# A four-layer transformer on one core: in the second layer the query and key projections are issued ahead of the weight turns

## The reference, cut to what matters

```python
# attention: 16 heads of 64, per sequence; a sparse causal mask
q, k, v = split(xn @ w_qkv)
attn = softmax(where(mask, q @ k.T * scale, -inf))
out  = (attn @ v) @ w_out
# ffn: 8 experts, each token weighted by its two best gates
scores = sigmoid(xn @ gate_w.T)
w_t    = scores where the expert is among the top 2 of scores + bias, else 0
out   += sum over e of square(relu((xn * w_t[e]) @ w_up[e].T)) @ w_down[e].T
```

## Time and profile before

| what | number |
|---|---|
| median of 3 runs | 2010.46 us (2008.64 to 2013.45) |
| the profiled execution | 2017.39 us, span 2015.5 us |
| mean granted TensorE clock | 0.961 |
| busy over the span | PE 91%, DVE 70%, ACT 60%, POOL 52% |
| the second layer's steps | about 434 to 1108 us of the span |

### The profile page before, as it was taken

One profiled execution on the slowest core, in us unless ns is written; L12 is line 12 of the kernel. 1 busy time (PEld: TensorE's weight loads), 2 busy tenths in 40 slices (PEclk: granted clock), 3 DMA queues, 4 the chain that ended last, 5 costly groups with the idle time before them and its releaser, 6 DMA issues.

```text
span 2015.5 us, 40795 instructions
## 1 busy us (share of the span) xinstructions
PE 1828.9 (91%) x13210; PEld 1346.1 (67%) x13210; DVE 1407.1 (70%) x4875; ACT 1206.3 (60%) x3496; POOL 1039.7 (52%) x1489
## 2 busy tenths in 40 slices
PE   5788787549999999999999899999998999999998
PEld 2555564337777777777777566666666777777776
DVE  6999974347677676777766766666665777777775
ACT  3445243246666666666665555555555787777885
POOL 3211354838888888887888311111113555555554
PEclk9889689869999999999999999999998999999999
DMA  6100014530311101110110000000000000000000
GB/s 189 34 1 2 2 25 116 94 93 20 126 28 28 27 18 33 28 28 27 18 33 12 21 1 1 1 1 1 1 1 1 5 4 7 7 7 7 7 2 12
DMA packets 74976, 53.66 MB, mean 27 GB/s; under 512 B 7056, under 2 KB 72976, under 8 KB 73872
## 3 DMA queue, kind: packets, MB, share of 16 engines
q1 hardware_dynamic: 69136, 46.73, 8.3%
q0 software_dynamic: 5632, 4.33, 1.6%
HBM read 40.30 MB, written 10.75 MB: 25 GB/s over the span
## 4 chain that ended last, share of the span: by engine, by line
PE 61%; DVE 11%; ACT 5%; issue 3%; POOL 2%; DMA 0%; POOLq 0%; DVEq 0%; ACTq 0%
PE bank L2243 4%; PE bank L1295 4%; PE bank L2230 3%; PE bank L1282 3%; PE bank L1270 3%; PE bank L2218 3%; PE bank L2215 2%; PE bank L1267 2%; PE bank L1806 2%; PE bank L1735 1%; PE bank L2195 1%; PE bank L2196 1%; PE bank L2197 1%; PE bank L2234 1%; DVE work L1956 1%
## 5 line engine op out<-in xcount | busy, mean ns | idle before, releaser
L2453 POOL TENSOR_TENSOR work<-work 128x128 f32<-128x128 f32 (+1 forms) x512 | 243.8, 508 | 223.9 <-DVE work L2387 223.7
L1603 POOL TENSOR_TENSOR work<-work 128x128 f32<-128x128 f32 (+1 forms) x512 | 248.0, 516 | 77.6 <-DVE work L1519 77.0
L1533 DVE SCALAR_TENSOR_TENSOR work<-bank,w_f 128x512 f32<-128x512 f32 x128 | 87.7, 690 | 112.6 <-PE bank L1318 69.8
L1394 ACT ACTIVATE l_squares_hi<-work 128x512 fp32r<-128x512 f32 x128 | 80.3, 628 | 122.1 <-PE bank L1329 90.2
L2392 DVE COPY work<-bank 128x384 f32<-128x384 f32 x256 | 134.2, 546 | 17.5 <-PE bank L2243 17.4
L1524 DVE COPY work<-bank 128x384 f32<-128x384 f32 x256 | 134.0, 545 | 16.6 <-PE bank L1295 16.6
L2298 ACT ACTIVATE work<-work 128x128 f32<-128x128 f32 x256 | 100.9, 394 | 60.6 <-DVE work L2383 60.6
L2299 ACT ACTIVATE work<-work 128x256 f32<-128x256 f32 x256 | 127.4, 498 | 0.0
L1384 ACT ACTIVATE work<-work 128x256 f32<-128x256 f32 x256 | 127.2, 497 | 0.0
L2382 DVE CUSTOM_DVE_ANT_0 work<-bank,mask 128x128 f32<-128x128 f32 x256 | 73.4, 287 | 74.0 <-PE bank L2218 74.0
L2090 POOL TENSOR_TENSOR work<-work,minus_half 128x4 f32<-128x4 f32 x8 | 8.5, 1060 | 224.5 <-DVEq L1952 224.5
(11 more groups left out here) (415 smaller groups left out, 5935.8 us busy)
## 6 DMA issues: line engine op xcount, KB each, us to landing
w_f<-gates SPq DMA_DIRECT2D x64, 256.0 KB, 5.0
w_l<-in_l SPq DMA_DIRECT2D x1, 3210.5 KB, 10.8
w_l<-in_l SPq DMA_DIRECT2D x2, 1540.0 KB
w_f<-in_f SPq DMA_DIRECT2D x1, 3072.0 KB, 13.9
x_sb<-in_x SPq DMA_DIRECT2D x4, 512.0 KB, 5.9
normed_rows<-work SPq DMA_DIRECT2D x1, 2048.0 KB, 9.3
even_experts<-x_sb SPq DMA_DIRECT2D x8, 256.0 KB, 3.6
residual<-x_sb SPq DMA_DIRECT2D x1, 2048.0 KB, 8.6
```

The lines of the kernel that those rows point to most:

```text
L1603: ins_ = pool.tensor_tensor(w, w, spread(rc[:, g % 2, u, q:q + 1], w.shape[1]), ALU.mult)
L2453: ins_ = pool.tensor_tensor(w, w, spread(rc[:, g % 2, u, q:q + 1], w.shape[1]), ALU.mult)
```

## The change

In PE's list for the second layer, project("q", s), the logits and project("k", s) stand behind weighted(s-3) and ahead of turned(s-2, 0), and the four turned units come together. Nothing else differs: the other engines' lists, the ring's order, the semaphores and their values are the same. The last layer has the same pipeline and keeps its order.

```diff
                     if 0 <= s - 3 < N:
                         weighted(s - 3)
-                    if 0 <= s - 2 < N:
-                        turned(s - 2, 0)
-                        turned(s - 2, 1)
                     if 0 <= s < N:
                         project("q", s)
-                    if 0 <= s - 2 < N:
-                        turned(s - 2, 2)
-                        turned(s - 2, 3)
                     if s >= 0 and (s + 1) % PAIRS == 0 and s + 1 < N:
                         logits((s + 1) // PAIRS)
                     if 0 <= s < N:
                         project("k", s)
+                    if 0 <= s - 2 < N:
+                        for u in range(UNITS):
+                            turned(s - 2, u)
                     if 0 <= s - 3 < N:
                         output(s - 3)
```

## The result

| | changed kernel | before | ratio |
|---|---|---|---|
| median | 2105.9 us (2101.96 to 2107.5, 4 runs) | 2011.13 us (2008.64 to 2013.45, 4 runs) | 1.0461, 95% interval 1.0441 to 1.0481 |
| profiled execution, span | 2104.54, 2102.7 us | 2017.39, 2015.5 us | |

Slower by 94.8 us, in the forecast's range of 2074 to 2112; 2095 was forecast, 84.4 us for the change. Times are medians.

A forecast was written before the change was run, and what follows sets the result against it. PE's list plus its waits was taken to bound the second layer. 54 plain steps x 1.14 = 61.6 and 7 logits steps x 3.25 = 22.8 make 84.4 us, on a median of 2010.5: 2095 us, range 2074 to 2112.

The forecast's parts named there:

- Where the time goes: PE's path from weighted to output in the second layer: 4.15 us against 3.01, as PE waits for DVE's heads_rest.
- Plain steps: The 54 second-layer steps with projections, transposes and output but no logits: +1.14 us each, 61.6 us in all.
- the row of step 64: Step without projections, already in the changed order: transposes to output 2.32 us, PE idle 0.80, clock 1.00.
- Switches: Changes between kinds of matmul on PE: 0 saved, bounds -5 to +6 us over 61 steps.
- What queues behind: DVE, POOL and ACT work after the delay in plain steps: hidden, no second wait, about 0.5 us to spare.
- Steps with logits: Seven steps where k waits for ACT's q copy and values for DVE's gates: +3.25 us each, 22.8 in all.
- The clock: PE's granted clock in the layer: stays at 1.00, nothing added to the sum; a rival had it fall, 3%.
- a fall in every step: Rival: transposes, wait and some 13 products run at 1.2 GHz in 61 steps, 189 us more, 2284; 3%.
- The range: Bounds of the forecast time, 2074 to 2112 us, from switches, logits steps, the chain's single row and run spread.
- The signs: What the profile after should show, such as PE idle ahead of output; wrong if the last layer's time changes.

The follow-up runs named there:

- e1: Changed kernel with heads_rest moved on DVE ahead of the copies of units 0 and 1; 2030.52 us, ratio to before 1.0092.
- e6: Changed kernel with unused matmuls in the seven steps with logits, four in the wait ahead of k and seven ahead of values; 2093.97 us.
- e2: Against the kernel before, only q moves ahead of the four turned units, with logits and k behind them; 2035.35 us, ratio 1.0118.
- e4: Kernel before, PE's order kept, with heads_rest moved on DVE behind the copies of units 2 and 3; 2068.44 us, ratio 1.0276.
- e5: Changed kernel with the logits behind the four turned units on PE, and behind k in the ring and on ACT; 2076.89 us, ratio 1.0324.
- e3: Changed kernel with turned units 0 and 1 kept ahead of q, units 2 and 3 behind k; 2026.56 us, ratio 1.0077.
- e10: Changed kernel with four unused matmuls in the wait ahead of k alone, in the seven steps with logits; 2099.35 us.
- e11: Changed kernel with seven unused matmuls in the wait ahead of values alone, in the seven steps with logits; 2097.33 us.

## Why the prediction was right, and where it was off

- *Where the time goes* held. Plain steps: +1.09 us measured, +1.14 said (q and k 1.49, as said; transposes to output 2.27 against 2.32, as the first copy follows 0.53 us behind them and not 0.59). 2.7 us too much over 54. Of the path 0.80 us are PE's wait, as in the earlier trace rows, not "some 1.0". That the row of step 64 could stand for all is the reason why the number was good.
- *Switches* cancel: said 0 within -5 and +6, measured 0.03 us a step in e1, 2 us.
- *What queues behind* held: no second wait in plain steps; values wait seven times.
- *Steps with logits*: said +3.25, measured +2.99. The 3.30 us between transposes and reciprocal, taken from the plain step of the earlier trace rows, are too long by 0.24. 0.06 of it is the first copy again. The other 0.18 is a short wait of the reciprocal for ACT's last exps: before, the exps end at 707.78 and the reciprocal starts at 707.82 (the earlier trace rows show the same wait at 0.45). In the changed kernel that step is later on DVE and the exps are done by then: the reciprocal stands 3.06 behind the transposes (693.08 - 690.02) and waits for nothing.
- *The clock* was the mis-sized term. It was put at nothing in the forecast, with 3% for a fall in every step at 189 us. It falls, but only in the seven steps with three waits, once in each and for about 3.4 us, and costs 7.9 us in this execution. The step of the argument that failed is the sentence that step 64 speaks against a fall. That held for a wait of 0.80 us, in 53 steps out of 53. It said nothing on a step with waits of 1.39, 0.80 and 1.98 us, though the same text had worked out that such steps come: it has more than a microsecond ahead of k and 2.3 ahead of values. Without the term the layer would have lost 79 us, 5 less than the 84.4 that were said, and with it 87: that the sum came so near is in part luck, as the two errors have opposite signs.
- *The range.* Its own terms add up to 28 us down and 14 up, 2067 to 2109, where it says 2074 to 2112. The measured 2105.9 lies in both.
- *The signs.* The last layer did not change: from its first values to its last it is 463.4 us long in both traces.
- The rule of the Trainium skill, that transposes don't count as work for the clock in the way other matmuls do (TensorE: Matmul & The Clock Gate, Part 4), was not seen to act here: in e6 twelve transposes and 0.8 us of idle PE stand in a row in every step and the layer's clock is 1.00. No run here separates transposes from other matmuls.
- 84.4 us said, 87 measured in the layer. Of the 94.8 between the medians 8 are left. They come from the choice of the profiled executions: that of before took 6.3 us more than its median, that of the changed kernel 1.4 less than its own. The 6.3 lie most likely ahead of this layer (its first values stand at 426.78, those of the other traces at 418 to 424); the 1.4 may be falls of the clock, since two of the other executions have a mean clock of 0.949 against 0.952. Neither is shown, as only one execution of each was profiled.

## What to carry over

When work was moved on the busiest engine here, its own cost stayed (0.03 us a step); look for what the moved work used to cover, and read on the partner engine which operation stands behind the one that now starts late. A tail or head of a pipeline, in which the covering work is missing, showed in the trace of before what the whole stage would do after. And an operation that nobody waits for yet should not stand in a queue ahead of one that is waited for: e1 got 75 us back by that.

## What the runs showed of the hardware

TensorE's clock fell with PE never idle for more than 2.4 us at a time and busy between the waits. What PE did in and around the seven steps with logits, and how often the clock went to 1.2 GHz there (for 3.4 us each time, once for 6.8 in e1):

| kernel | waits in the step with logits, us | falls in 7 steps |
|---|---|---|
| before, e2, e4 | 1.36 to 1.38 | 0 in each |
| e5 | 0.18, 1.71 | 1 |
| e3 | 0.80, 2.12 | 2 |
| e1 | 0.68, 2.36 | 4 |
| e10 | 0.46, 0.79, 1.98 | 4, behind the last |
| e11 | 1.39, 0.79, 0.35 | 4, behind the first |
| changed | 1.39, 0.80, 1.98 | 5 behind the last, 2 behind the first |
| e6 | 0.46, 0.79, 0.36 | 0 |

One wait of 0.79 us in each step of 11.1 us left the clock at 2.4 GHz in all plain steps. The same waits brought it down in some steps and not in others, so their length alone doesn't decide; that several waits in a step add up is a guess that these rows allow and don't show. Filling both long waits with matmuls that nothing uses kept it up, 7 times of 7.

DVE and GpSimd held each other up on certain operations. The same operation of DVE, x's rest (128x512, two inputs in SBUF), beside GpSimd's L1612 before, and in e1, where it was first:

```profile
574.71 1.28 POOL L1612 TENSOR_TENSOR l_squares_lo<-w_l,l_squares_hi 128x512 fp32r<-128x512 f32 x1
574.78 1.75 DVE L1492 TENSOR_TENSOR l_xn_lo<-work,l_xn_hi 128x512 fp32r<-128x512 f32 x1
```

```profile
571.65 0.68 DVE L1489 TENSOR_TENSOR l_xn_lo<-work,l_xn_hi 128x512 fp32r<-128x512 f32 x1
571.68 1.78 POOL L1609 TENSOR_TENSOR l_squares_lo<-w_l,l_squares_hi 128x512 fp32r<-128x512 f32 x1
```

Whoever came second, by 0.03 to 0.07 us, waited the other out: DVE ends 0.54 us behind GpSimd's end at 575.99, GpSimd takes 0.50 longer than its 1.28. The Trainium skill has the sharing (GPSIMD Engine Reference, section 1, Specifications, the table's line on SBUF interfaces: contention with DVE instructions with two SBUF inputs). The trace agrees; these rows show besides that the second one lost nearly the whole length of the first. The maxima, which read PSUM, keep their 0.42 us beside L1609 in e1 (at 572.81), and the copies, which do too, their 0.52 beside GpSimd's weights in the kernel before (at 579.23).
